# Geometric attention scores from fp32r high and low rows in one stacked product, with one scan for both prefix extremes

## What is computed

```
q = rope((LN(x) @ Wq) split in 8 heads of 32);  k = rope((LN(x) @ Wk) split in 2 heads), each for 4 heads
qp[t, h] = sum over d < 3 of q[t, h, d] * dirs[h, d]
kp[s, h] = sum over d < 3 of k[s, h, d] * dirs[h, d]
geo[h, t, s] = qp[t, h] * kp[s, h], -1e9 where s > t
geo_out = softmax(geo over s) @ v
out = (1 - scale[h]) * softmax attention + scale[h] * geo_out
```

## Time and profile before

| | |
|---|---|
| time, median of 3 runs (lowest, highest) | 466.85 us (465.57, 467.7) |
| the profiled execution's own time | 464.53 us |
| its span, first to last instruction | 462.6 us |
| mean granted TensorE clock, as a share of full speed | 0.919 |
| attention part | to about 277 us of the span |
| busy time in the span: TensorE, VectorE, ScalarE, GpSimd | 383.4, 331.9, 258.3, 152.0 us |

### The profile page before, as it was taken

How to read it: one execution, slowest core, us unless ns; L and a number is a source line. 1 busy time by engine, 2 the same in 40 slices (tenths; PEclk the granted TensorE clock), 3 DMA queues, 4 the chain that set the end, 5 groups by cost and what they waited for, 6 DMA issues and landing times. The chain is left out here.

```text
span 462.6 us, 7493 instructions
## 1 busy us (share of the span) xinstructions
PE 383.4 (83%) x2290; PEld 252.8 (55%) x2306; DVE 331.9 (72%) x865; ACT 258.3 (56%) x482; POOL 152.0 (33%) x161
## 2 busy tenths in 40 slices
PE   2578899999999999999997714778999999989795
PEld 1345455565554665555643302456777777768573
DVE  4374769877779787797877362568889898897742
ACT  1133676456775667756575222555675585755642
POOL 1221345334553335443341111133433333332310
PEclk9776999999999999999998566569999999999998
DMA  8930003000000000000000000000000000000001
GB/s 233 314 118 1 0 2 104 11 13 11 14 0 13 12 13 13 12 2 11 13 13 11 0 1 2 0 0 0 3 13 11 24 11 14 13 12 24 11 25 34
DMA packets 13642, 13.14 MB, mean 28 GB/s; under 512 B 2004, under 2 KB 12884, under 8 KB 13476
## 3 DMA queue, kind: packets, MB, share of 16 engines
q1 hardware_dynamic: 13604, 12.67, 9.1%
HBM read 10.57 MB, written 2.10 MB: 27 GB/s over the span
## 5 line engine op out<-in xcount | busy, mean ns | idle before, releaser
L884 POOL TENSOR_TENSOR c_h_lo<-c_hb,c_h_hi 128x512 fp32r<-128x512 f32 x32 | 40.8, 1274 | 72.0 <-ACT c_h_hi L927 66.7
L1022 PE MATMUL wide<-had,c_h_hi 128*128 128x512 f32 x128 | 54.0, 422 | 7.5 <-ACT c_q2T L938 7.5
L1022 PE MATMUL wide<-had,c_h_lo 128*128 128x512 f32 x128 | 51.2, 400 | 0.0
L1008 PE MATMUL wide<-c_q_T,w_tern_all 128*128 128x256 bf16 x256 | 38.3, 292 | 8.3 <-DVE c_hh L1120 6.9
L296 POOL TENSOR_TENSOR a_qk<-a_rot_c,a_rot_s 128x320 f32<-128x320 f32 x16 | 15.4, 962 | 72.6 <-DVE a_rot_s L677 72.6
L302 POOL TENSOR_TENSOR a_split_q<-a_qk,a_split_q 128x256 fp32r<-128x256 f32 x16 | 33.8, 2111 | 15.3 <-ACT a_split_k L394 15.3
L921 ACT ACTIVATE c_sl<-c_z 128x512 f32<-128x512 f32 x32 | 20.1, 628 | 29.4 <-DVE c_z L1111 29.3
L776 DVE TENSOR_TENSOR x_res<-x_res,bank 128x256 f32<-128x256 f32 x16 | 6.8, 422 | 40.9 <-PE bank L597 36.2
L1008 PEld LDWEIGHTS wide<-c_q_T,w_tern_all 128*128 128x128 bf16 x256 | 24.2, 103 | 20.7 <-DVE c_hh L1120 9.3
L586 PE MATMUL bank<-w_o,a_att 128*128 128x256 f32 x128 | 33.3, 405 | 1.9 <-issue 1.1
L563 PE MATMUL wide<-a_g_diag,a_row_sb 40*128 40x512 f32 x64 | 31.7, 615 | 2.6 <-DVE a_g_diag L696 2.6
(11 more groups left out here) (168 smaller groups left out, 1009.6 us busy)
## 6 DMA issues: line engine op xcount, KB each, us to landing
x_res<-in_x SPq DMA_DIRECT2D x4, 512.0 KB, 6.2
b_vT<-in_ctxT SPq DMA_DIRECT2D x16, 128.0 KB, 2.3
out<-c_yo SPq DMA_DIRECT2D x16, 128.0 KB, 1.7
w_raw_all<-in_wg SPq DMA_DIRECT2D x1, 1024.0 KB, 7.4
w_raw_all<-in_wu SPq DMA_DIRECT2D x1, 1024.0 KB, 9.8
w_raw_all<-in_wd SPq DMA_DIRECT2D x1, 1024.0 KB, 12.3
had_f<-in_h SPq DMA_DIRECT2D x1, 1024.0 KB, 4.9
w_o_raw<-in_Wo SPq DMA_DIRECT2D x4, 128.0 KB, 6.3
```

Source lines behind the costliest of these rows:

```text
L884: nc.gpsimd.tensor_tensor(h_lo[p][:, j::FQ, :], hb[j % 2][:, :].rearrange("c (m t) -> c m t", m=2), h_hi[p][:, j::FQ, :].bitcast(F32), ALU ...
L1008: mm = nc.tensor.matmul(dst[:, m * TOK:(m + 1) * TOK], w[:, k * FF + blk * P:k * FF + blk * P + P], q_T[p][:, k * TOK:(k + 1) * TOK], star ...
L1022: mm = nc.tensor.matmul(wide[:, 1 + i, m * 512:(m + 1) * 512], a[p][:, j + FQ * m, i * P:(i + 1) * P], had512[:, j, :], start=(j == 0 and ...
```

## The change

The same scores are computed from fp32r operands. An fp32 number is split into a high part, which fp32r holds, and the rest as a low part; with a high and a low row for each of qp and kp, all four partial products (high-high, high-low, low-high, low-low) are stacked in the contraction. Rows 0 to 7, 8 to 15, 32 to 39 and 40 to 47 of `stack` hold the parts of qp on one side and of kp on the other, rows 64 to 71 and 96 to 103 the high and low part of the row maximum against -1: 104 rows. `a_g_diag` grows to 104 rows and becomes fp32r. For the extremes `a_proj_d` also gets the negated kp (and qp) at rows 32 to 39, so that one maximum scan over 40 rows gives the prefix maximum of kp and of -kp. VectorE makes the high and low columns in stage `f`, TensorE transposes them, ScalarE copies them to `stack`, and the maximum is split by VectorE. The diff, cut to its core; what is left out are semaphore names and counts of start-up memsets, and the directions' constant, which gets its negated copy:

```diff
         mask_st = sb("mask_st", [P, 4 * P], BF16)
-        diag_mask = sb("diag_mask", [40, H * P])
+        diag_mask = sb("diag_mask", [104, H * P])
         pick_neg = sb("pick_neg", [40, H * P], F32R)
...
             split_k = sa("a_split_k", [P, 2 * KVH * 4 * DH], F32R)
-            dq = sa("a_dq", [P, 2 * H * 3])
-            proj_d = sa("a_proj_d", [P, 2 * H])
+            dq = sa("a_dq", [P, 4 * H * 3])
+            proj_d = sa("a_proj_d", [P, 128])
+            proj_v = [a[:, :].rearrange("t (a s y) -> t a s y", a=2, s=2)[:, :, :, 0:H] for a in proj_d]
+            dir_hl = sa("a_dir_hl", [P, 192], F32R)
             qkT = sa("a_qkT", [P, 1024], F32R)
...
             k_row = [r[:, 2 * P:3 * P] for r in row_sb]
-            cmax = sa("a_cmax", [8, P])
-            cmin = sa("a_cmin", [8, P])
+            stack = sa("a_stack", [104, 2, P], F32R)
+            cmax = sa("a_cmax", [40, P])
+            gm = sa("a_gm", [72, P])
             ra = sa("a_ra", [8, P])
             rb = sa("a_rb", [8, P])
-            g_diag = sa("a_g_diag", [40, H * P])
+            g_diag = sa("a_g_diag", [104, H * P], F32R)
             e_s = sa("a_e_s", [P, H * P])
...
             geo = wide[:, 2, :]
-            rows = scores[:, 0:3 * P]
...
-            names = ("st6 mv ve rstd xn t1 xT proj rot qk v hi lo dq dir tq qT s mx rows mrow grow cmx cmn "
+            names = ("st6 mv ve rstd xn t1 xT proj rot qk v hi lo dq dir tq qT s mx rows mrow grow stk hl cmx ghl "
                      "rab gm gd nm es geo eg pd pn vn ln inv att wo x1").split()
...
                 cut = lambda a: a[:, :].rearrange("r (h t) -> r h t", h=H)
-                return cut(g_diag[p]), spread(g_row[p][:, :], 1, H), cut(diag_mask)
+                return cut(g_diag[p]), spread(stack[p][:, 0, :].bitcast(F32), 1, H), cut(diag_mask)
...
                         need(act, A["gd"], u - 1)
-                        nc.scalar.copy(row_sb[p][0:8, :], rows[0:8, :]).then_inc(A["grow"], 1)
+                        nc.scalar.copy(row_sb[p][:, :], rows[0:40, 0:3 * P]).then_inc(A["grow"], 1)
+                        nc.scalar.copy(stack[p][0:64, :, :], rows[0:64, 3 * P:5 * P].rearrange("r (a t) -> r a t", a=2)).then_inc(A["stk"], 1)
                         need(act, A["grow"], u + 1)
...
                         need(pe, A["dir"], u + 1)
-                        nc.tensor.transpose(rows[0:8, P:2 * P], proj_d[p][:, 0:H], ident[:, :])
-                        nc.tensor.transpose(rows[0:8, 2 * P:3 * P], proj_d[p][:, H:2 * H], ident[:, :]).then_inc(A["rows"], 1)
+                        for a in range(2):
+                            nc.tensor.transpose(rows[0:40, (1 + a) * P:(2 + a) * P], proj_d[p][:, 64 * a:64 * a + 40], ident[:, :])
+                        need(pe, A["hl"], 4 * (u + 1))
+                        for a in range(2):
+                            mm = nc.tensor.transpose(rows[0:64, (3 + a) * P:(4 + a) * P].bitcast(F32R),
+                                                     dir_hl[p][:, 64 * a:64 * a + 64], ident_r[:, :])
+                        mm.then_inc(A["rows"], 1)
                     if f is not None:
...
                                              start=True, stop=True)
+                        need(pe, A["stk"], u + 1)
                         need(pe, A["gd"], u + 1)
                         for g in range(2):
-                            mm = nc.tensor.matmul(geo[:, g * 512:g * 512 + 512], k_row[p][:, :],
+                            mm = nc.tensor.matmul(geo[:, g * 512:g * 512 + 512], stack[p][:, 1, :],
                                                   g_diag[p][:, g * 512:g * 512 + 512], start=False, stop=True,
...
                         need(pe, A["mx"], u)
-                        need(pe, A["grow"], u)
+                        need(pe, A["stk"], u)
                         for j, sp in enumerate([split_q[p]] * 4 + [split_k[p]] * 4):
...
                 for p in range(2):
-                    nc.vector.memset(row_sb[p][:, 0:2 * P], 0.0).then_inc(s_init, 1)
-                    nc.vector.memset(k_row[p][0:32, :], 0.0).then_inc(s_init, 1)
-                    nc.vector.memset(k_row[p][32:40, :], -1.0).then_inc(s_init, 1)
+                    nc.vector.memset(proj_d[p][:, :], 0.0).then_inc(s_init, 1)
+                    nc.vector.memset(dir_hl[p][:, :].bitcast(F32), 0.0).then_inc(s_init, 1)
+                    for r in (slice(64, 96), slice(96, 104)):
+                        nc.vector.memset(stack[p][r, 0, :].bitcast(F32), 0.0).then_inc(s_init, 1)
+                        nc.vector.memset(stack[p][r, 1, :].bitcast(F32), -1.0).then_inc(s_init, 1)
                     nc.vector.memset(m_row[p][:, :].bitcast(F32), 0.0).then_inc(s_init, 1)
...
                         need(dve, A["gm"], u - 1)
-                        nc.vector.tensor_tensor_scan(cmax[p][:, :], k_row[p][0:8, :], k_row[p][0:8, :],
-                                                     k_row[p][0:8, 0:1], ALU.max, ALU.max).then_inc(A["cmx"], 1)
+                        nc.vector.tensor_tensor_scan(cmax[p][:, :], k_row[p][:, :], k_row[p][:, :],
+                                                     k_row[p][:, 0:1], ALU.max, ALU.max).then_inc(A["cmx"], 1)
...
                         u, p = m
-                        nc.vector.tensor_tensor_scan(cmin[p][:, :], k_row[p][0:8, :], k_row[p][0:8, :],
-                                                     k_row[p][0:8, 0:1], ALU.min, ALU.min).then_inc(A["cmn"], 1)
                         need(dve, A["cmx"], u + 1)
-                        nc.vector.tensor_tensor(ra[p][:, :], g_row[p][0:8, :], cmax[p][:, :], ALU.mult).then_inc(A["rab"], 1)
-                        need(dve, A["cmn"], u + 1)
-                        nc.vector.tensor_tensor(rb[p][:, :], g_row[p][0:8, :], cmin[p][:, :], ALU.mult).then_inc(A["rab"], 1)
+                        nc.vector.tensor_tensor(ra[p][:, :], g_row[p][0:8, :], cmax[p][0:8, :], ALU.mult).then_inc(A["rab"], 1)
+                        nc.vector.tensor_tensor(rb[p][:, :], g_row[p][32:40, :], cmax[p][32:40, :], ALU.mult).then_inc(A["rab"], 1)
                         need(dve, A["rab"], 2 * (u + 1))
+                        need(dve, A["ghl"], 2 * (u - 1))
+                        nc.vector.tensor_tensor(gm[p][64:72, :], ra[p][:, :], rb[p][:, :], ALU.max).then_inc(A["gm"], 1)
+                        need(dve, A["gm"], u + 1)
                         need(dve, A["gd"], u - 1)
-                        nc.vector.tensor_tensor(g_row[p][32:40, :], ra[p][:, :], rb[p][:, :], ALU.max).then_inc(A["gm"], 1)
-                        need(dve, A["gm"], u + 1)
+                        nc.vector.tensor_copy(stack[p][64:72, 0, :], gm[p][64:72, :]).then_inc(A["ghl"], 1)
+                        need(dve, A["ghl"], 2 * u + 1)
+                        nc.vector.tensor_tensor(stack[p][96:104, 0, :], gm[p][64:72, :], stack[p][64:72, 0, :].bitcast(F32),
+                                                ALU.subtract).then_inc(A["ghl"], 1)
+                        need(dve, A["ghl"], 2 * (u + 1))
+                        need(dve, A["stk"], u + 1)
                         need(dve, A["geo"], u - 1)
...
                         need(dve, A["dir"], u - 1)
-                        d3 = dirs[:, :].rearrange("t (h d) -> t h d", h=H)
                         qv = qk[p][:, :].rearrange("t (h d) -> t h d", h=NQK)
-                        dv = dq[p][:, :].rearrange("t (h d) -> t h d", h=2 * H)
-                        nc.vector.tensor_tensor(dv[:, 0:H, :], qv[:, 0:H, 0:3], d3, ALU.mult).then_inc(A["dq"], 1)
-                        nc.vector.tensor_tensor(
-                            dv[:, H:2 * H, :].rearrange("t (g i) d -> t g i d", g=KVH),
-                            spread(qv[:, H:NQK, 0:3], 2, REP),
-                            d3.rearrange("t (g i) d -> t g i d", g=KVH), ALU.mult).then_inc(A["dq"], 1)
-                        need(dve, A["dq"], 2 * (u + 1))
+                        signed = dirs[:, :].rearrange("t (s h d) -> t s h d", s=2, h=H)
+                        dv = dq[p][:, :].rearrange("t (a s h d) -> t a s h d", a=2, s=2, h=H)
+                        nc.vector.tensor_tensor(dv[:, 0], spread(qv[:, 0:H, 0:3], 1, 2), signed, ALU.mult).then_inc(A["dq"], 1)
+                        for g in range(KVH):
+                            r = slice(g * REP, (g + 1) * REP)
+                            nc.vector.tensor_tensor(dv[:, 1, :, r, :], spread(spread(qv[:, H + g, 0:3], 1, REP), 1, 2),
+                                                    signed[:, :, r, :], ALU.mult).then_inc(A["dq"], 1)
+                        need(dve, A["dq"], 3 * (u + 1))
                         need(dve, A["rows"], u - 1)
-                        nc.vector.tensor_reduce(proj_d[p][:, :], dv, AX.X, ALU.add).then_inc(A["dir"], 1)
+                        nc.vector.tensor_reduce(proj_v[p], dv, AX.X, ALU.add).then_inc(A["dir"], 1)
+                        need(dve, A["dir"], u + 1)
+                        plain = proj_v[p][:, :, 0, :]
```

(32 more changed lines are left out.)

## The result

The changed kernel takes 497.94 us (median of 4 runs, 496.58 to 500.14) against 466.21 us for the kernel before in the same comparison: a ratio of 1.069, 95% interval 1.063 to 1.075. The forecast was slower, at 474.1 us, with a range to 482.5; the kernel is slower by 31.7 us, over four times the 7.3 forecast. The two profiled executions have spans of 494.7 and 462.6 us. The feed-forward part is the same to 1 us (184.5 after, 185.3 before); its first instruction moves from 277.30 to 310.21, so the whole loss, 32.9 us, lies in the attention part.

A forecast was written before the change was run, and what follows sets the result against it. Bound: the loop of `a_att`, TensorE's output projection, then VectorE's list to the next `a_att`, with 0.71 us slack. 0.25 + 0.63 + 0.45 - 0.71 = 0.62 us in 14 rounds, +8.7, less 1.4: 474.1 us, range 466.0 to 482.5.

The forecast's parts named there:

- the shared access: VectorE and GpSimd excluding one another in SBUF: +0.45 us a round lost by VectorE, bounds 0 and 1.0.
- TensorE's saved work counted as 0 in the steady rounds: Geometric product in fp32r: about -1.2 us net a round, counted as 0 because transposes L576 wait for GpSimd's L306.
- VectorE, first half: From L685 to `a_g_diag`: one scan goes, a copy and a subtract come; `a_g_diag` starts +0.25 us later.
- VectorE, second half: Small instructions from L716 to L748, ahead of `a_xn` and `a_att`: +0.63 us a round, bounds +0.5 and +0.85.
- Rival (1): L302 gets the access ahead of `a_g_diag`; `a_att` 1.2 us later a round, 482.5 us; chance 0.14.
- ScalarE's added copy: Copy to `stack` ahead of cast L361: +0.28 us, covered by scan L663, so 0 in the sum.
- The early rounds: First three rounds, GpSimd not yet held by two sums: TensorE's gain taken as even with what VectorE adds.
- The last rounds: Last round with a geometric product, where L586 starts on the tail of L563: -1.4 us, once.
- (3): TensorE is the bound after all and its 17 us come in full: 450 us; chance 0.02.
- (5): New product isn't single-pass, nothing gained or lost on TensorE: 475.5 us; counted in the main case, no own chance.
- (2): Faster: small instructions at lower bound, no added GpSimd loss, `a_att` delay inside the slack: 464.0 us; chance 0.10.
- (4): Even: about 0.1 us a round lost, 1.4 us won back, 466.9 us; chance 0.14.

The follow-up runs named there:

- putting the work back: The changed kernel with its 104-row product read as fp32 again in place of fp32r: 480.37 us, ratio 1.024 to the kernel before.
- the small instructions alone: The kernel before with only the changed kernel's block of eight small VectorE instructions added, product still fp32 on 40 rows: 495.01 us, ratio 1.059.
- the product alone: The kernel before with only its 40-row geometric product in fp32r, low parts left out: 469.18 us, ratio 1.005.
- the `a_att`-first kernel: The changed kernel with `a_xn` and `a_att` straight after `a_g_diag`, and ScalarE's `a_e_g` ahead of the mix's logarithm: 466.66 us, ratio 0.995.
- a change of order alone: The kernel before, arithmetic untouched, with VectorE and ScalarE in the `a_att`-first order: 456.64 us, ratio 0.978.
- the two best versions with an fp32r product: Changed kernel, `a_att` first, high and low instructions on GpSimd: 461.27 us; kernel before, 40-row fp32r product plus six useless TensorE products: 462.77 us.

## Why the prediction was wrong

The direction and the mechanism on VectorE were right; the size was not. A little over half of the loss came by a mechanism that the prediction didn't have, and one term of the other half, the shared access, was too small.

**The step that failed: TensorE's saved work counted as 0 in the steady rounds.** The prediction had it as "about -1.2 us of work a round" and then "so I count this as 0". The work is indeed hidden: the transposes did wait for GpSimd. But work taken from a waiting TensorE, with the later start of the output projection, brought its clock down under the one group of products that the round waits for. Measured by putting the work back: 18.5 us of the profiled executions, 17.6 of the medians, about 21 by the ratios. In the other direction the falls can come without the saved work (the small instructions alone), so the cause is not the fp32r product by itself but what TensorE does over the round. What was shown: in the steady rounds the falls go when work or depth is added to TensorE with everything else in place, in five kernels out of five. What stays open is what sets off a fall, and why the product alone brings four and the whole change one in nearly every round. A rival that no run varies by itself is the length of the round, which is 14.26 us with the product alone and 15.34 with the whole change and so may let a fall come back at the same place of the next round or not. It can't be all of it: with the small instructions alone the falls went at an unchanged round of 15.07.

The Trainium skill, page "TensorE: Matmul & The Clock Gate", section "Part 1: The HAM clock gate", says that the clock is gated by how busy the array has been and has two levels. The trace agrees on the levels (0.50 and 1.00). The prediction named no term for the clock; in the kernel before it stood at 1.00 for the whole of 80 to 240 us, and the one edit to the product (469.18 us, clock 0.96) was enough to bring it down there.

**VectorE, first half.** Forecast +0.25 for the start of `a_g_diag`; measured 2.01 us behind the rotation against 1.73: +0.28. The copy took 0.22 as priced. Right.

**VectorE, second half.** Forecast +0.63 for the small instructions by themselves. With GpSimd idle (the `a_att`-first kernel) they take 1.09 us from the first multiply to the next instruction (153.74 to 154.83), against 0.41 before: +0.68. Right.

**The shared access: the mis-sized term.** Forecast +0.45. In the changed kernel the same block takes 1.71 us (151.23 to 152.94), 0.62 more than by itself: 0.49 of it in the first subtract (0.66 against 0.17), 0.13 in the first copy (0.30 against 0.17), each while one of GpSimd's low parts is being made. `a_xn` takes 0.78 against 0.41, 0.37 more, beside GpSimd's next multiply, the mix's `b_ev_in` (152.86 to 153.57), less the 0.18 of before. The prediction counted the two low parts, with part of each hidden, and not that third instruction. Together +0.81; the upper bound was 1.0. The sum is 0.28 + 0.68 + 0.81 - 0.71 = 1.06, and the output projection does start 1.05 later behind the rotation (6.97 against 5.92), where the forecast had 0.62. The small instructions alone bear this out: a round of 15.07 us at full clock, 0.81 above the 14.26 before. With the clock up the kernel takes 478 to 480 us, above the 474.1 and inside the range. The order of the two was as forecast: `a_g_diag` and the mix's sums first. Rival (1) did not happen: L305 began with `a_g_diag` at 149.42, and waited, 2.79 us long.

**The steady round's other terms.** ScalarE's added copy (0.36) and the two added transposes cost nothing, as forecast; the scan was cover enough. The start, put at 0 and at most 1, cost 0.8 to the first `a_mx`. The early rounds, taken as even, were not: with the clock up the third takes 15.22 us against 13.18. The last rounds gained more than the 1.4 us given: from the last `a_mx` to the feed-forward part 33.4 us against 36.8, of which a part is the clock, up in the changed kernel where it was down before.

**The rivals.** (3), TensorE as the bound, has no sign. (5) no: the product is single-pass, 0.70 us for two. (2), faster, and (4), even, did not happen. None of the five held what took half of the loss.

## What to carry to other kernels

Ahead of taking work off TensorE, ask what its clock will do: work that hides behind a wait is not worthless if the clock hangs on it, and the first thing to read after such a change is the granted clock under the products on the critical path. Small dependent VectorE instructions cost more than they take by themselves (0.68 us) where GpSimd works beside them (0.62 us more); put them where VectorE waits anyway, which took back 0.99 of 1.08 us. Before shortening an instruction, make it the last thing waited for: a change of order alone gave 2.2% (interval 1.4 to 2.9%), the lowest time here, where the two best versions with an fp32r product gave 1.3 and 1.4%. Those intervals overlap, so that it is better than these two is likely and not shown.

## What was not expected of the hardware

A TensorE product with more rows in its contraction, at the same length and with zeros in the added rows, kept the clock up where the 40-row one let it fall: 477.91 against 495.01 us, in one pair of kernels. Nor does the time busy rank the kernels by clock: in a round at full clock TensorE is busy for 12.3 of 14.59 us with `a_att` first, where the clock never falls from 80 to 240 us, and for 13.5 of 15.07 with the small instructions alone, where it falls in seven rounds of eleven.
